# First batch of a cross attention: sums of four exponential tiles by GpSimd and an accumulating DMA, one cycle of nine tiles, key and query loads in pieces

## Time and profile before

| | |
|---|---|
| profiled execution | 2017.9 us, span 2016.1 us |
| median of three runs | 2020.58 us (2014.73 to 2026.13) |
| TensorE busy | 1919.1 us, 95% of the span |
| VectorE | 1221.2 us, 61% |
| ScalarE | 882.5 us, 44% |
| GpSimd | 793.8 us, 39% |
| the cross attention's loop | from 535.9 us (first exponential) to about 1478 us |
| DMA | 211.04 MB, 105 GB/s on average |

### The profile page before, as it was taken

How to read it: one execution, slowest core, us unless ns; L and a number is a source line. 1 busy time by engine, 2 the same in 40 slices (tenths; PEclk the granted TensorE clock), 3 DMA queues, 4 the chain that set the end, 5 groups by cost and what they waited for, 6 DMA issues and landing times.

```text
span 2016.1 us, 26457 instructions
## 1 busy us (share of the span) xinstructions
PE 1919.1 (95%) x10152; PEld 1268.9 (63%) x10152; DVE 1221.2 (61%) x2279; ACT 882.5 (44%) x1587; POOL 793.8 (39%) x705
## 2 busy tenths in 40 slices
PE   6999999989999999999999999999969999999992
PEld 5876665667655555555444545544438999888991
DVE  5565543237677777777778779768654444444433
ACT  3212322222365666666556556546724443333431
POOL 3002200000177777777667657656012222322112
PEclk9999999999999999999999999999979999999996
DMA  6102433574533031312425334422234454444316
GB/s 247 42 1 99 155 107 131 184 220 126 161 96 85 17 76 47 95 43 59 100 65 131 75 93 113 121 48 74 79 111 137 126 138 125 112 136 101 104 22 187
DMA packets 119070, 211.04 MB, mean 105 GB/s; under 512 B 10608, under 2 KB 28672, under 8 KB 118864
## 3 DMA queue, kind: packets, MB, share of 16 engines
q1 hardware_dynamic: 108416, 185.39, 31.2%
q0 software_dynamic: 9440, 21.86, 5.6%
q10 hardware_dynamic: 1088, 2.10, 0.3%
HBM read 147.15 MB, written 62.42 MB: 104 GB/s over the span
## 4 chain that ended last, share of the span: by engine, by line
PE 85%; DVE 10%; DMA 2%; ACT 1%; issue 1%; SPq 0%; POOL 0%; ACTq 0%; POOLq 0%; DVEq 0%
PE banks L1070 36%; PE banks L1236 11%; PE banks L1325 11%; PE banks L1206 10%; PE banks L1225 9%; DVE max L1499 7%; PE banks L1254 5%; PE banks L1076 2%; DMA k_parts<-out_lo 1%; DMA wv_raw<-in_wv_t 1%; DVE stats_y L1707 0%; PE banks L1144 0%; DVE src_lo L1369 0%; DVE wq_lo L1375 0%; ACT src_hi L1754 0%
## 5 line engine op out<-in xcount | busy, mean ns | idle before, releaser
L1499 DVE TENSOR_REDUCE max<-banks 128x1 f32<-128x512 f32 x1024 | 627.6, 683 | 163.3 <-PE banks L1206 162.3
L1969 POOL TENSOR_TENSOR probs_sum<-probs_sum,probs_add 128x512 f32<-128x512 f32 x464 | 581.9, 1285 | 299.8 <-PE banks L1236 299.8
L1206 PE MATMUL banks<-k_stack,q_stack 98*128 98x512 f32 x1024 | 427.8, 425 | 3.7 <-DVE max L1499 2.7
L1847 ACT ACTIVATE probs_sum<-banks 128x512 f32<-128x512 f32 x512 | 264.6, 604 | 296.6 <-PE banks L1225 296.1
L1225 PE MATMUL banks<-q_stack,k_stack 98*128 98x512 f32 x1024 | 377.0, 398 | 2.0 <-ACT probs_sum L1847 2.0
L1206 PEld LDWEIGHTS banks<-k_stack,q_stack 98*128 98x128 f32 x1024 | 192.1, 188 | 190.8 <-issue 82.7
L1847 ACT ACTIVATE probs_add<-banks 128x512 f32<-128x512 f32 x512 | 272.6, 613 | 0.0
L1225 PEld LDWEIGHTS banks<-q_stack,k_stack 98*128 98x128 f32 x1024 | 191.9, 188 | 61.8 <-ACT probs_sum L1847 10.3
L2011 POOL DMA_INDIRECT y_rows<-eo,tok x40 | 81.5, 2037 | 216.4 <-DVE eo L1700 168.9
L1236 PE MATMUL banks<-probs_sum,v_grp 128*32 128x512 f32 x1024 | 139.9, 607 | 0.0
L1687 DVE TENSOR_TENSOR hid_lo<-hid,hid_hi 128x640 fp32r<-128x640 f32 x64 | 52.8, 826 | 140.6 <-ACT hid_hi L1912 140.6
(11 more groups left out here) (233 smaller groups left out, 2785.2 us busy)
## 6 DMA issues: line engine op xcount, KB each, us to landing
k_stack<-k_parts SPq DMA_DIRECT2D x144, 256.0 KB, 4.8
w_raw<-in_L_ffn_w SPq DMA_DIRECT2D x16, 2048.0 KB, 9.7
q_stack<-q_parts SPq DMA_DIRECT2D x48, 256.0 KB
v_grp<-v_rows SPq DMA_DIRECT2D x48, 256.0 KB, 3.1
raw<-in_ctx_t SPq DMA_DIRECT2D x8, 1024.0 KB, 6.7
k_parts<-out_hi SPq DMA_DIRECT2D x32, 256.0 KB, 2.5
k_parts<-out_lo SPq DMA_DIRECT2D x32, 256.0 KB, 2.9
v_rows<-pre SPq DMA_DIRECT2D x32, 256.0 KB, 2.3
```

Source lines behind the costliest of these rows:

```text
L1206: nc.tensor.matmul(out, queries_of(t)[:, j, tile_of(k)], keys_of(t)[0:STK + SHIFT, j, mc * HALF:(mc + 1) * HALF], start=True, stop=True) \
L1499: V.reduce_max(max4[:, tiles_of(t), :, :][:, k, j, mc:mc + 1], bank(bank_of["max", t, mc, k, j]), AX.X) \
L1847: S.activation(probs_of(t, s)[:, j, :], bank(bank_of["score", t, s, j]), ACT.Exp, scale=SCALE) \
L1969: done = G.tensor_tensor(a[:, j, :], a[:, j, :], b[:, j, :], ALU.add)
```

## The change

In the first batch except its last four context tiles (`by_fours`), denominators are taken over four context tiles at a time. GpSimd adds the odd tile onto the even one, now with a wait for each head (`add_head`), as before twice for four tiles. It then issues one DMA that adds the first pair's sum (1 MB in SBUF) onto the second's (`add_four`), one block after the second addition was issued. The denominators of the four are put four blocks after the second pair. The second batch keeps its pairs.

All exponential tiles come from one cycle of nine. A tile written by an odd context tile is reused five context tiles later, head by head as GpSimd finishes, one written by an even one thirteen later, after the accumulating DMA or the denominators. Room for the three more comes from one `y_nat` in place of two, from a smaller scratch of the software DMA (2048 bytes a partition instead of the default), and from tiles that are laid elsewhere. With one `y_nat`, the rows of the first batch's second half are fetched after the first half's have been stored. `num_c` gets a second buffer. Loads of keys and queries are cut into single DMAs that are issued over the blocks (one key piece a block in turns 1 to 6, else up to three; up to two query pieces). The loads for folding weights (`load_fold`, turn 1) and the rest (`load_xwo`, turn 3) come later than before; so does the fold (turn 2). Inversions are spread 0, 2, 2, 1, 1, 1, 1 over the blocks after `copy_den`.

```diff
-        probs = [[put(f"probs_{name}{i}", [P, HG, HALF]) for i in range(n)] for name, n in (("sum", 3), ("add", 3))]
+        probs = [put(f"probs{i}", [P, HG, HALF]) for i in range(9)]
...
-        y_nat = [put(f"y_nat{i}", [P, HT, D]) for i in range(NH)]
+        y_nat = put("y_nat", [P, HT, D])
...
-        num_c = put("num_c", [P, HALF])
+        num_c = [put(f"num_c{i}", [P, HALF]) for i in range(2)]
...
+        def by_fours(t, s):
+            return t * MT + s < B * NG * MT - FOUR
+        def four_of(t, s):
+            return (t * MT + s) // FOUR % FOUR
...
@@ divide @@
                 elif g == NG - 1 and t < LAST:
+                    if not b and h:
+                        start_side(fetch_rows(b, h))
                     start_side(rows_of(b, h))
...
@@ loads_after_scores @@
-            if t == last_of[stay] and s % HT == HT - 1:
-                load_k(stay + 2, s // HT)
-            if s == MT - 1:
-                load_q(t + PLACES)
+            if t == last_of[stay] and s % HT == HT - 1 and stay + 2 < len(stays):
+                key_loads.extend((stay + 2, s // HT, i) for i in range(PARTS))
+            for _ in range(1 if 0 < t < B * NG - 1 else PARTS):
+                if key_loads:
+                    do("load_k", *key_loads.pop(0))
+            if s == MT - 1 and t + PLACES < len(turns):
+                query_loads.extend((t + PLACES, i) for i in range(PARTS + 1))
+            for _ in range(2):
+                if query_loads:
+                    do("load_q", *query_loads.pop(0))
...
@@ the loop, after the numerators of (turn, s), (turn, s + 1) and denominators(clock) @@
                 if not end:
-                    do("add_pair", turn, s + 1)
-                    pending.append((clock + 1, turn, s + 1))
-                invert(4 if turn == LAST else (0, 2, 2)[s // 2] if s < 6 else 1, 1)
-                if g == NG - 2 and s == 2:
+                    while fours:
+                        do("add_four", *fours.pop())
+                    if by_vector(turn, s + 1):
+                        do("add_pair", turn, s + 1)
+                    else:
+                        for j in range(HG):
+                            do("add_head", turn, s + 1, j)
+                    if not by_fours(turn, s):
+                        pending.append((clock + 1, turn, s + 1))
+                    elif s % FOUR == 2:
+                        fours.append((turn, s + 1))
+                        pending.append((clock + 4, turn, s + 1))
+                invert(4 if turn == LAST else 0 if clock == divisions_from[0] else
+                       2 if clock < divisions_from[0] + 3 or turn == B * NG - 1 else 1, 1)
+                if g == NG - 2 and s == 2 and (b or not h):
                     start_side(fetch_rows(b, h))
...
@@ probs_of, probs_before @@
-            tiles = probs[s % 2]
-            return tiles[(t * MT + s) // 2 % len(tiles)]
+            four, place = divmod(t * MT + s, FOUR)
+            return probs[(four - (0, 3, 4, 7)[place]) % len(probs)]
-            earlier_step = t * MT + s - 2 * len(probs[s % 2])
+            earlier_step = t * MT + s - (13 if s % 2 else 5)
...
@@ ScalarE: score @@
-                    if s0 % 2 == 0:
+                    if s0 % FOUR == 0 and by_fours(t0, s0):
+                        act.wait_ge(*fours_added[four_of(t0, s0)][t0, s0 + 3])
+                    elif s0 % 2 == 0:
                         act.wait_ge(*den_summed[t0, s0 + 1])
                     elif by_vector(t0, s0):
                         act.wait_ge(*last_pair_added[t0, s0])
-                    else:
-                        act.wait_ge(*pair_added[t0, s0])
+                if before and before[1] % 2 and not by_vector(*before):
+                    act.wait_ge(*pair_added[(*before, j)])
...
@@ GpSimd @@
-            def add_pair(t, s):
-                if not by_vector(t, s):
-                    a, b = probs_of(t, s - 1), probs_of(t, s)
-                    pool.wait_ge(*exp_done[t, s, HG - 1])
-                    pool.wait_ge(*num_summed[t, s - 1])
-                    for j in range(HG):
-                        done = G.tensor_tensor(a[:, j, :], a[:, j, :], b[:, j, :], ALU.add)
-                    done.then_inc(pair_added.sem, 1)
+            def add_head(t, s, j):
+                a, b = probs_of(t, s - 1), probs_of(t, s)
+                pool.wait_ge(*exp_done[t, s, j])
+                pool.wait_ge(*num_summed[t, s - 1])
+                G.tensor_tensor(a[:, j, :], a[:, j, :], b[:, j, :], ALU.add).then_inc(pair_added.sem, 1)
+
+            def add_four(t, s):
+                pool.wait_ge(*pair_added[t, s, HG - 1])
+                G.dma_start(probs_of(t, s - 1)[:, :, :], probs_of(t, s - 3)[:, :, :], accum_op=ALU.add) \
+                    .then_inc(fours_added[four_of(t, s)].sem, 16)
...
@@ SyncE: fetch_rows @@
-                if b:
-                    sp.wait_ge(*x2_out[h][b - 1, h])
-                elif not h:
+                if h:
+                    sp.wait_ge(*x2_out[h - 1][b, h - 1])
+                elif b:
+                    sp.wait_ge(*x2_out[NH - 1][b - 1, NH - 1])
+                else:
                     sp.wait_ge(*folds_summed[()])
...
-    nc = _bacc.Bacc("TRN2", target_bir_lowering=False, num_devices=1)
+    nc = _bacc.Bacc("TRN2", target_bir_lowering=False, num_devices=1, dynamic_dma_scratch_size=2048)
```

More of the change, by code:

```diff
@@ L57 @@
 TILES_Y = 2
+FOUR = 4
+PARTS = 3
 PIECES_Y = B * NT // TILES_Y
@@ L208, in program @@
         head_w = put("head_w", [P, NG, DH])
+        earlier = put("earlier", [P, P])
         lane_no, col_no = put("lane_no", [P, P], I32), put("col_no", [P, COLS], I32)
@@ L242, in program @@
         att = [put(f"att{i}", [P, D]) for i in range(2)]
+        put.at = context_base - 4 * P - 2 * 4 * HALF
+        pre = [put(f"pre{i}", [P, HALF]) for i in range(2)]
         assert put.at <= context_base
@@ L254, in program @@
         xe_hi, xe_lo = (put(f"xe_{n}", [P, NC, CAP], F32R) for n in ("hi", "lo"))
-        xg = [put(f"xg{i}", [P, D]) for i in range(2)]
+        xg = [put(f"xg{i}", [P, D]) for i in range(NS)]
         assert put.at <= context_base
@@ L637, in load_k @@
             if stay < len(stays):
-                do("load_k", stay, c)
+                for i in range(PARTS):
+                    do("load_k", stay, c, i)
         def load_q(t):
             if t < len(turns):
-                do("load_q", t)
+                for i in range(PARTS + 1):
+                    do("load_q", t, i)
         def load_v(stay, c):
@@ L742, in side @@
             return True
-        divisions, pending, later = [], [], []
+        divisions, pending, later, fours, divisions_from = [], [], [], [], [0]
         clock = 0
@@ L825, in second_stack @@
             do("one_rows", 1)
[L826 to L829, removed]
+            query_loads.extend((2, i) for i in range(PARTS + 1))
+            key_loads.extend((1, c, i) for c in range(MCH) for i in range(PARTS))
             do("zero_counts")
@@ L1155, in fold @@
                 out = free_bank("fold")
-                pe.wait_ge(*xwo_in[()])
+                pe.wait_ge(*fold_in[()])
                 pe.wait_ge(*const_in[()])
-                by_column_groups(out, [(router_pad[:, c, :], y_nat[0][:, c, :]) for c in range(NC)]) \
+                by_column_groups(out, [(router_pad[:, c, :], y_nat[:, c, :]) for c in range(NC)]) \
                     .then_inc(folds_summed.sem, 1)
@@ L1241, in denominators_of @@
             def denominators_of(t, s):
-                if s == 1:
+                begun = s == (3 if by_fours(t, 0) else 1)
+                if begun:
                     free_bank("den", t)
@@ L1254, in denominators_of @@
                         done = nc.tensor.matmul(bank(DEN)[j * DH:(j + 1) * DH, :], ones[:, 0:DH], tile[:, j, :],
-                                                start=s == 1, stop=s == MT - 1 and tile is tiles[-1])
+                                                start=begun, stop=s == MT - 1 and tile is tiles[-1])
                 done.then_inc(den_summed.sem, 1)
@@ L1260, in rows_first @@
                 pe.wait_ge(*xo_added[b, h, k, EARLY])
-                accumulate(out, [(identity[:, :], y_nat[h][:, k, :])], stop=False)
+                accumulate(out, [(identity[:, :], y_nat[:, k, :])], stop=False)
             def rows(b, h, k, part):
@@ L1541, in rows @@
             def rows(b, h, k, part):
-                row = y_nat[h][:, k, :]
+                row = y_nat[:, k, :]
                 dve.wait_ge(*xo_summed[b, h, k, part])
@@ L1851, in copy_num @@
                 act.wait_ge(*num_summed[t, MT - 1])
-                if t:
-                    act.wait_ge(*divided[t - 1, HT - 1])
-                S.activation(num_c[:, :], bank(NUM), ACT.Copy).then_inc(num_copied.sem, 1)
+                if t > 1:
+                    act.wait_ge(*divided[t - 2, HT - 1])
+                S.activation(num_c[t % 2][:, :], bank(NUM), ACT.Copy).then_inc(num_copied.sem, 1)
             def copy_den(t):
```

111 lines of the change are left out of this document (61 added, 50 removed).

## The result

The changed kernel takes 1996.11 us in the median of four runs (1994.56 to 1997.19) for 2022.84 of the kernel before; the ratio is 0.9873, its 95% interval 0.9841 to 0.9905. Run again beside other kernels it took 1997.60, ratio 0.9878 (0.9860 to 0.9897). The forecast was 1995. The profiled execution took 1995.04 us, its span is 1993.4, 22.7 less than before.

What follows compares the result with a forecast made beforehand. TensorE was taken as the bound. Against the profiled 2017.9 us, -27.0 + 1.0 + 0.5 + 1.0 = -24.5 gave 1993.4, or 1996.1 from the median; forecast 1995 us, own range 1988 to 2003, overall 1987 to 2017.

Steps and rivals of the forecast that it cites:

- The passes: TensorE, first batch: 33 denominator passes in place of 64, at 0.87 us each 27.0 us less; bounds 0 and 30.1.
- VectorE: VectorE's maxima and inversion fit the block shortened to 6.06 us, by 0.6 us, or 0.1 with two inversions.
- GpSimd: GpSimd's two-block work, 10.54 us plus 1.7 to issue the accumulating DMA, is 12.2 and hidden in 12.99.
- The lower bound: Issue of the accumulating DMA on GpSimd: at least 0.59 us as a plain direct DMA, 0.83 with four times the pieces.
- the rival: GpSimd becomes the bound: issue of 5.0 us, kernel 2074 us; decides from 2.45, slower than before from 3.3; chance 0.07.
- The landing: Accumulating 1 MB DMA lands in 11 us, may take 18.1 before the odd exponentials reuse its source tile: hidden.
- The handover: Second block of turn 8: four passes in place of one, bank copy between the last two; 1.0 TensorE, 0.5 VectorE.
- One `y_nat`: Second half's rows fetched only after the first half's store, possibly stopping VectorE: 1.0 us, bounds 0 and 11.8.
- The rival that ate half the gain: Uncovered fetch costs 11.8 us on VectorE and TensorE, four passes in one block cost 2: 2006 us; chance 0.16.
- the tail: Shorter software DMA ring could hold up GpSimd's DMAs at the start and ahead of the experts: 0 taken, up to 2.
- the fetch: Loading the second half's rows into the single `y_nat`; a late landing stops VectorE's maxima, then TensorE: 1.0 us.
- the idle half microsecond: VectorE idles in turn 8's handover block and is short in none that could be named: 0.5 us.

Runs made afterwards that it cites:

- The operation added once: Changed kernel with one more GpSimd operation of an addition's size ahead of each accumulating DMA: 1995.68 us; with three such operations: 2071.57 us.
- the kernel with pairs: Changed kernel with denominators by pairs everywhere, 128 passes and no accumulating DMA, all else kept: 2017.46 us, ratio 0.9981 to the kernel before.
- the kernel with fours to turn 11: Changed kernel with fours to the end of turn 11 but its last four tiles, weights' fold one block later: 1991.67 us, ratio 0.9851.
- two deliberate overloads: Changed kernel with each accumulating DMA issued two blocks later: 2141.55 us; changed kernel with three more GpSimd operations ahead of each DMA: 2071.57 us.
- the kernel with fours to turn 13: Changed kernel with fours to the end of turn 13 but its last four tiles: 1991.21 us, ratio 0.9853 to the kernel before.

## Why the prediction was right

**The passes.** 0.87 a pass was predicted, 0.86 is measured, in turns 3 to 7 at 54.9 - 51.45 = 3.45 us for four passes. 784 matmuls, as counted. Turn lengths were forecast as 52.0 because I took a mean of seven turns that held the turn with the weights' fold (58.9) for the length of all.

**VectorE.** It fits by the margin that was worked out: in the block after 894.33 it was idle 0.62 before its first maximum, the figure forecast being 0.6. In blocks with two inversions it was 0.21, the forecast 0.1.

**GpSimd.** The sum of two blocks holds, but the issue was mis-sized: 0.87 us (0.81 to 0.95) for my 1.7. A direct accumulating DMA costs at most 0.28 more than the plain direct one of 0.59, so the 1.10 that I took from scatter less gather is not the price of accumulating here; what makes it up in the indirect form no run shows. The lower bound, 0.59 to 0.83, was nearer. The operation added once (nothing) and thrice (74 us more than the changed kernel, 76 worked out) shows the threshold of the rival; it was real and 1.45 us away.

**The landing.** 10.0 us (6.9 to 14.4) for 11, deadline about 18: right, and shown by moving the issue, 8 to 12 us for one block and 144 for two. Of the engines' time, the queue took 273.1 us for 54.30 MB (13.7% of the span) less 112.9 for 21.86 before: 160 for 32.4 MB, 4.9 a MB, a little under the forecast's 5.2 to 6.9. The Trainium skill's 4.4 us for 1 MB (DMA: Bandwidth & Descriptors, Anatomy of one DMA) lies below even the shortest, 6.9: the trace does not bear it out for accumulating.

**The handover.** Forecast 1.0 + 0.5. The timeline after turn 7 shows the four passes:

```profile
964.38 2.76 PE L1298 MATMUL banks<-probs,ones 128*32 128x512 f32 x24
966.10 0.13 PEld L1298 LDWEIGHTS banks<-probs,ones 128*32 128x32 f32 x4 [0.30 <-issue]
967.21 0.60 ACT L1908 ACTIVATE den_c<-banks 128x512 f32<-128x512 f32 x1 [3.84 <-PE banks L1298]
967.86 0.16 PEld L1298 LDWEIGHTS banks<-probs,ones 128*32 128x32 f32 x8 [1.62 <-ACT den_c L1908]
```

Three run back to back, the copy follows, and the fourth starts only after it: its weights would have been due half a pass after the last ones loaded, at 966.10 + 0.43 = 966.53, and came at 967.86: 1.3 us. **One `y_nat`**, 1.0 in the forecast, cost nothing: no wait for it stands in the trace. The rival that ate half the gain by it falls.

**What the sum balanced.** Between pairs and fours, turns 8 to 15 take 492.6 and 501.2 us. Of the 8.6 more, 1.7 are two passes that fall there instead of in turn 7, 3.8 an output product that moved from turn 7 to turn 8 (with pairs turn 7 takes 58.7, the turns before it 54.9), and 3.1 are a loss. 1.3 of it is the bank's copy. Of the other 1.8, two waits of TensorE for ScalarE's exponentials (0.8 at 1036.7, 0.5 at 1189.8), which the kernel with pairs doesn't have in turns 8 to 12, would make 1.3; why they arise there, and the last 0.5, stays open. Another 1.7 went in turn 2, which was in no step of the prediction: behind the fold's 24 small matmuls (8 columns each, 662.25 to 665.1) TensorE's granted clock fell to 0.66 for 5 us, with no pause ahead of it. With pairs the same matmuls left it at 1.00. These windows are of TensorE in the changed kernel:

```profile
660.00:665.00 5.00, 4.90 (x33) 1.00 0.26 52
665.00:670.00 5.00, 5.00 (x28) 0.66 0.00 0
```

In the kernel with fours to turn 11 the fold stands one block later, and its clock fell too; turn 2 took 56.8 us for 57.1, where 55.4 (58.84 with pairs, less 3.45) would have been without a loss:

```profile
670.00:675.00 5.00, 5.00 (x40) 0.87 0.90 182
675.00:680.00 5.00, 5.00 (x20) 0.79 0.16 33
```

In the changed kernel a denominator pass stands behind the small matmuls and none behind the fold's first product, a block earlier; here it is the other way round, and the clock falls in both. So the place of the pass doesn't explain it, and the cause stays open.

The same size of loss comes and goes between executions of one kernel. In turn 14 TensorE pauses for 1.7 us in both profiles of the changed kernel. In the first its clock falls after that and the turn takes 55.1 us, in the second it stays and the turn takes 53.45. The windows, first profile, then second:

```profile
1370.00:1375.00 5.00, 5.00 (x30) 0.73 0.00 0
...
1370.00:1375.00 5.00, 5.00 (x33) 1.00 0.00 0
```

So -26.7 became about -21.9 in the loop (22.5 by the traces), plus 1.7 in the tail and less 1.9 ahead of the loop, where the runs scatter by about 3 (first exponential at 532.6 to 535.9 us in thirteen of the fourteen profiles, 530.3 in the other). The sum of 24.5 was within 2 us of the spans' 22.7 with two terms that no row shows (the fetch, the idle half microsecond) and three that it lacked (turn 2's clock, the 1.8 in turns 8 to 12, the tail, for which it had named up to 2 and taken 0). The number was better than its parts, and that is luck.

## What to carry to other kernels

Where TensorE is the bound with engines beside it at 61 to 77%, price a removed group by the step between groups, and list the room of each neighbour in the new, shorter block; here the forecasts of 153 and 76 us for two deliberate overloads came out at 144 and 74. The same edit is worth less where the neighbours' queues are mixed: it gave 0.70 us a pass in the first batch and 0.2 to 0.3 in the second, where part of the gain went into pauses of TensorE and the lower clock after them. A transfer that is wanted four blocks later may be slow, but its deadline moves with the blocks, and missing it costs every block.

## What the hardware showed that was not expected

- A direct accumulating DMA of 1 MB within SBUF costs GpSimd 0.87 us to issue and lands in 6.9 to 14.4 us; at a DMA share of 0.87 in the mean it still lands in 10.1 (median). 31 of them, and another 31 MB beside them, left TensorE's turns as long as without.
- VectorE operations of four elements a partition took 0.91 to 1.33 us beside GpSimd's additions in six cases in the kernel with fours to turn 13, most of the others 0.16 to 0.17. In the loop of the changed kernel none of the 39 took over 0.46.
- After pauses of 1.7 to 8 us, and once behind 24 small matmuls without a pause, TensorE's granted clock was 0.50 to 0.73 over 5 us; sixteen numerator matmuls then took 3.64 us for 1.92. It does not fall each time: after the same pause of 1.7 us it fell in one execution and stayed at 1.00 in another, a difference of 1.6 us.
